# Four graph layers in one kernel: another order in the head, in layer 0's norms, in the scales and at the end

## What is computed

```
layer 0: out = sum_k As[k] @ x @ w[node, k] + b,  As = [I, A, 2 A A - I]
         (weights per node from a 16-wide embedding)
layer 1: attention over neighbours with adj > 0.5, then elu
layer 2: (adj + I) @ (x W' + b) / deg
layer 3: v[:, 0] = intervention; three times:
         effects = adj @ v;  v = relu([v, effects] W1' + b1) W2' + b2
```

## Time and profile before

| what | value |
|---|---|
| median of three runs | 1060.19 us |
| the profiled execution | 1058.48 us |
| its span in the profile | 1056.7 us |
| TensorE busy | 1026.8 us (97%) |
| VectorE busy | 727.3 us (69%) |
| ScalarE busy | 422.6 us (40%) |
| GpSimd busy | 536.2 us (51%) |
| share of the chain that ended last | TensorE 82%, VectorE 8%, GpSimd 3% |
| granted TensorE clock | 0.994 of full |

### The profile page before, as it was taken

How to read it: one execution, slowest core, us unless ns; L and a number is a source line. 1 busy time by engine, 2 the same in 40 slices (tenths; PEclk the granted TensorE clock), 3 DMA queues, 4 the chain that set the end, 5 groups by cost and what they waited for, 6 DMA issues and landing times.

```text
span 1056.7 us, 18773 instructions
## 1 busy us (share of the span) xinstructions
PE 1026.8 (97%) x6922; PEld 493.9 (47%) x6922; DVE 727.3 (69%) x1751; ACT 422.6 (40%) x1081; POOL 536.2 (51%) x623
## 2 busy tenths in 40 slices
PE   7999999999999999999999999999999999999994
PEld 3446444434443444344345555555554545455542
DVE  4876565677557765775674899988667776767556
ACT  4632233333334343534423555446345422231633
POOL 0004487547456766775671757578864233323300
PEclk9999999999999999999999999999999999999998
DMA  9930000000000000000010121212212100000022
GB/s 368 399 122 1 1 2 2 1 2 1 1 1 2 1 2 2 1 1 2 1 41 1 41 81 41 81 41 81 80 41 81 40 1 1 3 1 22 21 60 60
DMA packets 14657, 45.65 MB, mean 43 GB/s; under 512 B 960, under 2 KB 9280, under 8 KB 10080
## 3 DMA queue, kind: packets, MB, share of 16 engines
q1 hardware_dynamic: 14560, 44.39, 11.4%
HBM read 40.19 MB, written 4.19 MB: 42 GB/s over the span
## 4 chain that ended last, share of the span: by engine, by line
PE 82%; DVE 8%; POOL 3%; issue 3%; ACT 2%; DMA 2%; SPq 0%; POOLq 0%; ACTq 0%; DVEq 0%
PE PS L743 33%; PE PS L872 20%; PE PS L916 18%; PE PS L728 2%; DMA BW<-at_in 2%; PE PS L729 2%; PE PS L730 2%; DVE BW L1187 1%; DVE T L1190 1%; PE PS L737 1%; ACT T L1035 1%; PE PS L735 1%; PE PS L736 1%; DVE X L1190 1%; PE PS L897 1%
## 5 line engine op out<-in xcount | busy, mean ns | idle before, releaser
L743 PE MATMUL PS<-BW,S 128*128 128x512 fp8e4 x1792 | 403.4, 379 | 4.0 <-DVE T L1190 2.0
L743 PEld LDWEIGHTS PS<-BW,S 128*128 128x128 f16 x1792 | 169.5, 98 | 210.7 <-issue 15.8
L872 PE MATMUL PS<-WZ,R 64*128 64x512 f16 x1536 | 198.7, 377 | 3.3 <-ACT T L1035 3.3
L1035 ACT ACTIVATE T<-PS,SM 128x128 f32<-128x128 f32 x384 | 112.5, 365 | 207.3 <-DVE X L1190 137.6
L1735 POOL TENSOR_TENSOR T<-T 128x128 f32<-128x128 f32 (+1 forms) x192 | 126.8, 660 | 125.3 <-ACT T L1035 114.8
L1190 DVE SCALAR_TENSOR_TENSOR X<-PS,SM,X 128x128 f32<-128x128 f32 x320 | 109.7, 343 | 38.0 <-PE PS L872 37.8
L872 PEld LDWEIGHTS PS<-WZ,R 64*128 64x128 f16 x1536 | 69.2, 94 | 107.2 <-issue 25.4
L916 PE MATMUL PS<-BW,S 128*128 128x512 fp8e4 x512 | 115.4, 379 | 0.1
L872 PE MATMUL PS<-WZ,T 64*128 64x512 f16 x768 | 103.8, 376 | 0.0
L1735 POOL TENSOR_TENSOR S<-R,S 128x512 f16<-128x512 f32 x48 | 57.5, 1212 | 89.3 <-ACT S L1035 89.3
L1190 DVE SCALAR_TENSOR_TENSOR T<-PS,SM,T 128x128 f32<-128x128 f32 x256 | 87.9, 343 | 21.6 <-PE PS L872 21.6
(11 more groups left out here) (217 smaller groups left out, 1505.3 us busy)
## 6 DMA issues: line engine op xcount, KB each, us to landing
WZ<-a_in SPq DMA_DIRECT2D x16, 1024.0 KB, 4.8
BW<-at_in SPq DMA_DIRECT2D x8, 1024.0 KB, 18.5
R<-at_in SPq DMA_DIRECT2D x7, 1024.0 KB, 13.3
out<-X SPq DMA_DIRECT2D x16, 256.0 KB, 2.3
X<-x_in SPq DMA_DIRECT2D x3, 1024.0 KB, 20.7
T<-w_in SPq DMA_DIRECT2D x1, 1536.0 KB, 15.5
R<-at_in SPq DMA_DIRECT2D x2, 512.0 KB, 4.9
SM<-sm_in SPq DMA_DIRECT2D x1, 520.5 KB, 17.9
```

The source lines that it names most:

```text
L743: m = e.matmul(o, stile(h, t, c), Bm[:, t, block(j)], start=(t == 0 and h == 0), stop=(last and t == NT - 1 and h == 1))
L872: m = e.matmul(bank(b0 + q), halves[kd][zh][r, :], WZ[r, wh, kd, block(g)], start=(i == 0), stop=(i == 8))
L1035: return e.activation(o, i, f, **kw)
```

## The change

- Head: `E1` 0 to 3 stand further forward among the `R` steps, one at a time. `nb` alternates between its two partition groups and waits once, for both banks.
- Layer 0's norms, chunks 0 to 2: `rs` and the first `apply` at (u, 3), the second at (u, 4), the third at (u + 1, 0), the fourth and `sum` at (u + 1, 1), with u = 4c + 4. `mean` and `row_a` move to (6,2), (10,2), (13,2), `row_b` to (6,4), (10,4), (13,4). For chunks 0 and 1 layer 1's steps (`addrow`, `sq`, `var`, `rs`, `apply`, `split`) come one unit later. Chunk 3 stays.
- Scales: the first is cut in 0 and 1, at (2,1) and (2,3); the two large operations stand alone at (3,1) and (3,3); the rest is at unit k = 1 of layer 2.
- Checks: the maximum on VectorE is gone; ScalarE takes a Relu with a sum in its place, ahead of Sign.
- End: pairs of blocks share `var3`, the root (`root3`, now a step of its own) and `rs3`, the last pair too; blocks 10 and 11 of the last product's order go to GpSimd as well; block 13 is squared in one piece and summed on VectorE.

```diff
@@ -83,8 +83,9 @@
-HEAD = ([("R", jt) for jt in range(13)]
-        + [("E1", 0), ("E1", 1), ("R", 13), ("E1", 2), ("E1", 3), ("R", 14), ("R", 15), ("dg",)]
+HEAD = ([("R", jt) for jt in range(9)]
+        + [("E1", 0), ("R", 9), ("R", 10), ("E1", 1), ("R", 11), ("R", 12), ("E1", 2), ("R", 13), ("E1", 3), ("R", 14), ("R", 15)]
+        + [("dg",)]
         + pieces("P1", 0) + [("E1", 4), ("E1", 5), ("wm",), ("E1", 6), ("E1", 7), ("E1", 8)]
@@ -104,12 +105,20 @@
         at(u, 2, ("var", 0, c))
-        at(u, 3, ("rs", 0, c), ("apply", 0, c, 0), ("apply", 0, c, 1))
-        at(u, 4, ("apply", 0, c, 2), ("apply", 0, c, 3), ("sum", c))
-        if c == 3:
+        at(u, 3, ("rs", 0, c), ("apply", 0, c, 0))
+        at(u, 4, ("apply", 0, c, 1))
+        if c < 3:
+            at(u + 1, 0, ("apply", 0, c, 2))
+            at(u + 1, 1, ("apply", 0, c, 3), ("sum", c))
+
+            u += 1 if c < 2 else 0
+            at(u + 1, 2, ("mean", c), ("row_a", c))
+            at(u + 1, 4, ("row_b", c))
+        else:
+            at(u, 4, ("apply", 0, c, 2), ("apply", 0, c, 3), ("sum", c))
             u += 4
-        at(u + 1, 1, ("mean", c), ("row_a", c))
-        at(u + 1, 3, ("row_b", c))
+            at(u + 1, 1, ("mean", c), ("row_a", c))
+            at(u + 1, 3, ("row_b", c))
         for j in range(4):
@@ -120,9 +129,11 @@
         at(k // 2, 1 + 2 * (k % 2), ("xs", 3 + k))
-    at(2, 3, ("scales", 0))
-    at(3, 1, ("scales", 1))
-    at(3, 2, ("scales", 2))
+    at(2, 1, ("scales", 0))
+    at(2, 3, ("scales", 1))
+    at(3, 1, ("scales", 2))
+    at(3, 3, ("scales", 3))
+    at(17, 0, ("scales", 4), ("scales", 5))
     for u in range(16):
@@ -218,16 +229,21 @@
     for n, s, jj, h in ((6, 1, 0, 33), (6, 1, 1, 34), (6, 4, 0, 41), (6, 4, 1, 42), (6, 5, 0, 43), (6, 5, 1, 44), (6, 6, 0, 44),
-                        (6, 6, 1, 45), (7, 1, 0, 47), (7, 1, 1, 48), (7, 4, 0, 52), (7, 4, 1, 53), (7, 5, 0, 54), (7, 5, 1, 55)):
+                        (6, 6, 1, 45), (7, 1, 0, 47), (7, 1, 1, 48), (7, 4, 0, 52), (7, 4, 1, 53)):
         on(h, ("F", *ending(n, s, jj)), ("sq", 3, *ending(n, s, jj)))
-    for n, s, h in ((6, 1, 36), (6, 4, 43), (6, 5, 46), (6, 6, 47), (7, 1, 49), (7, 4, 54), (7, 5, 56)):
+    def outs(n, s):
+        return [("out", *ending(n, s, jj)) for jj in range(2)]
+
+    for n, s, h in ((6, 1, 36), (6, 4, 43), (6, 5, 46), (6, 6, 47), (7, 1, 49)):
         u = ending(n, s, 0)
-        on(h, ("var3", *u, 2), ("rs3", *u, 2), ("out", *u), ("out", *ending(n, s, 1)))
-    u, v = ending(7, 6, 0), ending(7, 6, 1)
-    between[55] = [("F", *u)]
-    w = half[56]
-    half[56] = [("sq", 3, *u), *w[:2], ("F", *v), ("sq", 3, *v), ("var3", *u, 1), ("rs3", *u, 1), *w[2:], ("out", *u),
-                ("var3", *v, 1), ("rs3", *v, 1), ("out", *v)]
+        on(h, ("var3", *u), ("root3", *u), ("rs3", *u), *outs(n, s))
+
+    r, (u, v), (x, y) = ending(7, 4, 0), [ending(7, 5, jj) for jj in range(2)], [ending(7, 6, jj) for jj in range(2)]
+    on(54, ("var3", *r), ("root3", *r), ("F", *u), ("sq", 3, *u), ("rs3", *r), *outs(7, 4))
+    on(55, ("F", *v))
+    between[55] = [("F", *x), ("sq", 3, *v), ("var3", *u)]
+    on(56, ("root3", *u), ("rs3", *u), *outs(7, 5), ("F", *y), ("sq", 3, *x), ("sq", 3, *y), ("var3", *x), ("root3", *x),
+       ("rs3", *x), *outs(7, 6))
     for g in range(2):
...
@@ -629,14 +646,14 @@
                     held[buf] = x[1:]
-                elif x[0] in ("var", "var3"):
+                elif x[0] in ("var", "root3"):
                     VARN[norm_key(x)] = len(VARN)
-        REDN = {x: n for n, x in enumerate(y for y in SQN if y[0] < 3 or not order3(*y[1:]) < 14)}
+        REDN = {x: n for n, x in enumerate(y for y in SQN if y[0] < 3 or order3(*y[1:]) > 12)}
         ORDER3 = [ending(n, s, jj) for n in (6, 7) for s in ENDS for jj in range(2)]
@@ -645,11 +662,11 @@
-            return order3(c, j) < 8 or order3(c, j) in (12, 13)
+            return order3(c, j) < 8 or 10 <= order3(c, j) < 14
-            return order3(c, j) < 14
+            return order3(c, j) < 13
@@ -810,12 +827,13 @@
                     e.wait_ge(s_b2b, 2)
-                    for h in range(2):
-                        e.wait_ge(s_u1, 5 + h)
-                        for t in range(8):
+                    e.wait_ge(s_u1, 6)
+                    for t in range(8):
+                        for h in range(2):
                             m = e.matmul(bank(4 + h)[:, t * C:t * C + C], embt[h][:, t * 128:(t + 1) * 128], nbias[h],
                                          start=True, stop=True)
-                        m.then_inc(s_nbm, 1)
+                            if t == 7:
+                                m.then_inc(s_nbm, 1)
                 elif kind == "wm":
@@ -1044,7 +1062,7 @@
                     act_e2(e, step[1])
-                elif kind == "scales" and step[1] == 0:
+                elif kind == "scales" and step[1] == 1:
                     e.wait_ge(s_xc, NT)
@@ -1083,12 +1101,14 @@
                         e.wait_ge(s_sq, SQN[L, c, j])
+                        if order3(c, j) == 15:
+                            e.wait_ge(s_red, REDN[(3, *ORDER3[13])] + 1)
                     elif SQPREV[L, c, j] is not None:
                     fn(four(sq_buf(L, c, j)), xpart(c, j), ACT.Square).then_inc(s_sq, 1)
-                elif kind in ("var", "var3"):
+                elif kind in ("var", "root3"):
                     L, c, j = (*norm_key(step), 0)[:3]
-                    m = step[3] if L == 3 else 1
+                    m = 2 if L == 3 else 1
                     e.wait_ge(s_var, VARN[norm_key(step)] + 1)
@@ -1167,13 +1187,16 @@
                     if it:
-                        e.wait_ge(s_cnt, it)
+                        e.wait_ge(s_over, it)
                     fn(junk, Bm[:, it, :], ACT.Copy, accum_out=cnt[:, it:it + 1]).then_inc(s_cnt, 1)
                 elif kind == "sgn":
+
                     it = step[1]
-                    e.wait_ge(s_nr, it + 1)
-                    if it:
-                        e.wait_ge(s_sign, it)
+                    e.wait_ge(s_land, 16 * (it + 1))
+                    e.wait_ge(s_nr, 1)
+                    e.wait_ge(s_cnt, it + 1)
+                    fn(junk, rowt, ACT.Relu, bias=nr[:, it:it + 1], accum_out=over[:, it:it + 1]).then_inc(s_over, 1)
+                    e.wait_ge(s_over, it + 1)
                     fn(rowt, rowt, ACT.Sign, bias=nr[:, it:it + 1], accum_out=sg1[:, it:it + 1]).then_inc(s_sign, 1)
...
@@ -1389,10 +1412,6 @@
                 e.wait_ge(s_sc, 1)
-                for t in range(2):
-                    e.wait_ge(s_hh, 2 + t)
-                    stt(e, hat[:, 1, t:4:2, :], BD[:, t::2, :], cs[:, cRho64 + t:cRho64 + t + 1], hat[:, 0, t:4:2, :],
-                        ALU.mult, ALU.subtract).then_inc(s_hl, 1)
@@ -1409,17 +1428,25 @@
                     qmax = fr[:, 1:2]
-                    if step[1] == 1:
+                    if step[1] == 0:
+                        e.wait_ge(s_flr, 1)
+                        fc(ts(e, col(cQmin), fr[:, 2:3], -1.0, None, ALU.mult))
+                        fc(e.reciprocal(col(cIQ), col(cQmin)))
+                        fc(ts(e, pair(cRho64), pair(cNG), 1e-30, None, ALU.max))
+                        fc(e.reciprocal(pair(cRho64), pair(cRho64)))
+                        continue
+                    elif step[1] in (2, 3):
+                        t = step[1] - 2
+                        e.wait_ge(s_hh, 2 + t)
+                        stt(e, hat[:, 1, t:4:2, :], BD[:, t::2, :], cs[:, cRho64 + t:cRho64 + t + 1], hat[:, 0, t:4:2, :],
+                            ALU.mult, ALU.subtract).then_inc(s_hl, 1)
+                        continue
+                    elif step[1] == 4:
                         scales_b(qmax)
                         continue
-                    elif step[1] == 2:
+                    elif step[1] == 5:
                         scales_c()
                         continue
-                    e.wait_ge(s_flr, 1)
-                    fc(ts(e, col(cQmin), fr[:, 2:3], -1.0, None, ALU.mult))
-                    fc(e.reciprocal(col(cIQ), col(cQmin)))
-                    fc(ts(e, pair(cRho64), pair(cNG), 1e-30, None, ALU.max))
-                    fc(e.reciprocal(pair(cRho64), pair(cRho64)))
                     fc(ts(e, pair(cRho64), pair(cRho64), col(cQmin), 1.5, ALU.mult, ALU.mult))
@@ -1466,18 +1493,19 @@
                 elif kind == "var3":
-                    c, j, m = step[1:]
-                    if summed_by_act(c, j):
-                        e.wait_ge(s_sq, SQN[3, c, j + m - 1] + 1)
-                    else:
-                        e.wait_ge(s_red, REDN[3, c, j] + 1)
+                    c, j = step[1:]
+                    for i in (j, j + 1):
+                        if summed_by_act(c, i):
+                            e.wait_ge(s_sq, SQN[3, c, i] + 1)
+                        else:
+                            e.wait_ge(s_red, REDN[3, c, i] + 1)
                     r = order3(c, j) // 2
```

(33 more changed lines are left out.)

## The result

The changed kernel takes 1062.58 us (median, 1061.06 to 1063.88) where the kernel before takes 1058.87 (1057.97 to 1060.27), eight runs each: a ratio of 1.0033, 95% interval 1.0022 to 1.0044. It is slower, by 3.7 us. The profiled execution took 1062.71 (span 1060.9) against 1058.48 (1056.7), so the two traces are 4.2 apart.

What follows compares the result with a forecast made beforehand. TensorE, busy 97% of the span, was taken as the bound, so only shortened waits count. Gains 10.6 less losses 9.0 gave net -1.6 us: median 1058.6 from 1060.19, range 1052.5 to 1063.3.

Steps and rivals of the forecast that it cites:

- −2.7 + 9.0 = +6.3: Layer 0's and 1's norms: moving the means of chunks 0 and 1 gains 2.7 us, new waits lose 9.0.
- 10.6 forecast: Whole kernel: gains of head 1.57, nb 0.25, layer 3 scales 2.08, means of chunks 0 and 1 2.7, end 4.0 us.
- The slower side: Whole kernel: a measured time above 1062.3 us, given a chance of 0.19.
- the rival that was given for it: Units 8 and 9: all eight dx and t1 late by about 1 us through bank 1; 1063.3 us, chance 0.20.
- 5.7 + 3.3 = 9.0: TensorE's losses in us: 5.7 at chunk 2's mean, 3.3 from chunk 0's layer 1 norm one unit later.
- the shrunk turns: Chunk 2's mean: two turns between sum and mean become one, so TensorE waits 3.7 us, the lower bound.
- the backlog: GpSimd, unit 12 on: chunk 1's splits, one unit later, delay its adds, making chunk 2's mean 5.7 us late, not 3.7.
- The term for chunk 0 in units 8 and 9: Chunk 0's layer 1 norm in unit 8 delays dx and t1: 4.2 us less 0.94, loss 3.3 (0 to 5.5).
- The third: Wait at dx 13 behind chunk 0's moved layer 1 norm: VectorE done about 335.4, TensorE ready at 334.5, 0.9 us.
- the pace of 0.104 may be a floor: Head, nb: at 64 columns alternation may not beat 0.104 us per instruction; 0.5 taken from 0 to 1.66, net 0.25.
- proof against it: Chunk 2's mean waiting under 3 us, no new wait in unit 8, or ScalarE showing as a releaser in layer 2.
- its signs: Old waits gone at t1, scales and end, about 0.5 at P1 0; new waits at chunk 2's mean (4 to 6 us), unit 8.

Runs made afterwards that it cites:

- E1: The kernel before with only the head's E1 0 to 3 moved forward among the R steps: 1057.95 us against 1058.86 (0.9993).

## Why the prediction was wrong

| part | forecast | alone on the chip |
|---|---|---|
| `E1` forward | −1.57 | −0.9 |
| `nb` | −0.25 | −2.1 |
| scales | −2.1 | −2.2 |
| checks | 0 | 0 |
| end | −4.0 | −3.8 |
| norms and means | −2.7 + 9.0 = +6.3 | +12.0 |
| sum | −1.6 | +3.0 (whole: +3.7) |

The gains were sized well in sum: 10.6 forecast with the means of chunks 0 and 1, 8.5 for the rest together and 2.7 read at the means. In part that is luck: `nb` gave 1.8 more than its 0.25, and `E1` less than its 1.57. The slower side came true, but not by the rival that was given for it: the eight `dx` and `t1` aren't all late, their waits in unit 8 and 9 stay few.

**The step that failed is the sum of the losses, "5.7 + 3.3 = 9.0": a wait of TensorE was priced at its length.** The mechanisms behind both terms were right. The mean of chunk 2 waits 6.34 (5.7 forecast), 4.03 of it by the shrunk turns and about 2.3 by the backlog, as reckoned (3.7 and 2.0). But behind it the granted clock fell to half, and that cost another 2.7, shown by the run that filled the wait. The earlier trace rows had no wait long enough to show this. The trace had signs that could have been asked for: behind the 2.06 near the end the granted clock is 0.70, behind `nb` 0.56, and the first 32 matmuls, behind 5.53 of idle time and while the adjacency lands, take 8.85 where 32 take 7.08 elsewhere:

```profile
5.53 8.85 PE L795 MATMUL PS<-BW,S 128*128 128x512 fp8e4 x32 [5.53 <-DVE BW L1187]
```

The granted clock stands at 1.00 in that last place, so why they are slow isn't shown. The Trainium skill (TensorE: Matmul & The Clock Gate, Part 1: The HAM clock gate) states that an idle TensorE drops to half clock and that the point of the change varies from run to run; the traces agree on both: 6.34, 5.69, 4.03 and 3.25 were each followed by a fall, while behind the same 1.94 in unit 8 it fell in two profiled executions and not in three.

The term for chunk 0 in units 8 and 9 came out at 5.1 of waits (0.51, 1.94, 1.47, 0.60, 0.22, 0.40, where the clock held) against 4.2. The third was forecast as 0.9. In the profile of the changed kernel the fall of the clock stands in for it, so the shift from turn (8,1) to (9,1), 4.9, is the same either way: here the clock is no cost of its own. Turn (9,1), where the last two of the waits lie, takes 7.13 where an undisturbed one takes 6.27. That makes 5.8 by the starts of turns, more than the listed waits.

Two smaller things were left out. Turn (13,1) has a new wait of 0.84 behind chunk 1's norm in unit 12. By the starts of turns the losses are 9.0 at the mean, 5.8 less 1.2 for chunk 0 and 1.0 in turn (13,1): 14.6, where 9.0 were forecast. The means of chunks 0 and 1 gain 3.0 by the same reading, which leaves 11.6 of the 11.8 that the new norms cost between the traces. In waits and clock: 0.64 + 2.7 at the mean, 0.84 in turn (13,1) and 5.8 - 4.2 = 1.6 in units 8 and 9 make 5.8, beside the 5.7 by which the norms were mis-sized. And the gain of `nb` was taken near its floor, "the pace of 0.104 may be a floor": it isn't, at 64 columns alternation brings the 0.104 down to 0.060 each. That is 1.7 times as fast, within the "up to twice" that the prediction cites.

None of the things happened that the prediction named as proof against it, and its signs came true in the main (the mean's wait, 6.34, a little over the 4 to 6 given): the list of signs had none for the clock.

## What to carry to other kernels

- A new wait of TensorE costs its length and, where it was long here, a stretch at half clock: about 1.7 us behind a wait of 4.0 and 2.7 behind 6.3; behind the same wait of 1.94 it fell in some executions only, and behind 2.30 at one of two places. Add it to the sum, unless an engine that is late anyway sets the time of what follows.
- Moving one of two recurring bursts by a whole unit can put it onto the other. Look at what already stands where a step is moved to, per engine, before pricing the step itself; one half of such a move may cost more than its share. Here undoing chunk 2 gave back 3.7 of 12.0, and chunk 0's move alone cost 9.1.
- Parts that gain and a part that loses come apart only if they are timed one by one: the same change without its norms runs in 1050.4.

## What the runs showed that was not expected

- 32 matmul instructions of 16 rows and 64 columns in f32 take 3.39 us on one partition group after the other and 2.00 on alternating ones. Behind the first form the granted clock fell in four profiled executions of five (0.56 and 0.59 from 84 to 88 us in the kernel before), though TensorE had not waited there; behind the second it stayed at 1.00 in all nine. Up to `P2` 0 the fall cost 0.07 to 1.8 us, since GpSimd is late there anyway.
- The same wait of 1.94 in the same place was followed by half clock in some executions and by full clock in others, and the stretch up to the fourth turn behind took 28.15 either way.
- Three multiplications of 128 x 512 on VectorE in a row took 1.60 each beside GpSimd's additions, against 0.69 alone.
